# Cross-attention and RWKV block on one core: the permutation of the scan's output, on the moving read or on the PSUM write

## The chip, the cores and the metric

The kernel runs on one core of a Trainium2 chip, in one launch. The metric is the device time of an execution in microseconds, as a median over runs. Differences under 2% count as no change.

## What is computed

Two layers run one after the other for each of B = 4 batches. The first is a cross-attention with a small MLP, the second one is an RWKV block: a time mix with a recurrent scan over 256 tokens, then a channel mix. What the change touches is the output of the scan, which is then normalised per head. Cut to that part (b, l, e are batch, token and channel; h = 32 heads of s_ = 8 channels j):

```python
def step(s, rkvw):
    r_t, k_t, v_t, w_t = rkvw
    a = k_t[..., :, None] * v_t[..., None, :]
    out = jnp.einsum('bhi,bhij->bhj', r_t, u * a + s)
    s = a + w_t[..., :, None] * s
    return (s, out)
_, out = jax.lax.scan(step, s0, rkvw)
og = jnp.moveaxis(out, 0, 1).reshape(b, l, h, s_)
m = og.mean(-1, keepdims=True)
va = ((og - m) ** 2).mean(-1, keepdims=True)
og = ((og - m) / jnp.sqrt(va + 1e-05)).reshape(b, l, e) * gn_w + gn_b
x1 = x + og * g @ Wo.T
```

## The kernel before

All arithmetic around the change is in f32. Channels are 256 = 2 chunks of 128 partitions (index c), tokens are 256 = 2 row tiles of 128 (index a). The work is written as a list of steps, in an order set out by hand (ORDER, a string of stream names and counts): attention steps (maxima, exponentials, their products with V) of all batches are woven with the four "tails", one for each batch, a tail being the rest of the first layer and the whole second layer. Every engine walks the same list and takes its part of each step; semaphores order the engines among themselves. TensorE therefore runs its units strictly in the order of the list.

A tail unit writes one of two PSUM banks (pW), used in turn. A unit may start when the reader of the unit two places earlier has done with its bank (claim).

Around the change the steps are these. VectorE runs the scan as first-order recurrences (L897), VectorE and GpSimd multiply by the receptance r, and unit wkv (L622) sums over the channel i of every head on TensorE. That sum comes out with partitions (j4, h), that is four of the eight j with 32 heads each, in two halves jj, and tokens along the free axis. ScalarE copies it into the tile T (L778). Unit ojT then turns it around: its output has tokens on the partitions and the 256 channels along the free axis, in the order (h, j) that the rest of the layer uses. It does this with matmuls whose stationary operand is the data and whose moving operand is the identity, into one bank. For each row tile two matmuls put the diagonal term VT there (L632, plain 128x128 transposes, the first one clearing), and two more add the scan's halves (L635), where the channel order has to be changed from (j, h) to (h, j). VectorE then reads the bank: it sums each head's eight channels (gsum, L1099) and subtracts the mean (L1101, which releases the bank). ScalarE squares (L708), VectorE makes the variance and its inverse root (L1005, L1008, L904 to L915), and the layer goes on with the products of Wo.

What stands behind ojT on TensorE differs by batch. In batch 0 it is the transposes of Z of the next batch's tail (unit zT, L422) and then that tail's up projection (L549, with the down projection L558 behind it). In batches 1 and 2 the transposes zT of the next tail stand directly ahead of ojT and the up projection behind it. In batch 3 it is the last matmuls of the gate (L414). Tiles are named by the program: pW is the pair of banks, `four` holds VT, T holds the scan's sum, ident is the identity.

Of the kernel before, what the change touches and what calls it, by code (L numbers as in the profile page):

```python
# [7 lines left out]
P = 128  # L8
# [7 lines left out]
B, TQ, TC, E = 4, 256, 512, 256  # L16
# [7 lines left out]
H, S = 32, E // 32  # L24
# [133 lines left out]
def build(nc, hT, x, mask, cols, rows, ident_in, bsum_in, bfull_in, pick_in, w_kq, w_vo, w_up, w_down,  # L158
          w_maa1, w_maa2, w_td1, w_td2, w_sq, out):
    ctx = ExitStack()  # L160
    with ctx:
# [9 lines left out]
        ident = sb("ident", [P, P])  # L171
# [222 lines left out]
        def _(pe):  # L394
            mm = nc.tensor.matmul
# [31 lines left out]
            for step in STEPS:  # L427
# [48 lines left out]
                elif kind == "unit":  # L476
# [60 lines left out]
                    elif name == "zT":  # L537
                        pe.wait_ge(did["z"], b + 1)
                        transposes(name, b, X.Z)
                    elif name[:2] == "up":  # L540
                        if name == "up0":
                            taken(pe, "zT", b)
                            if b == 0:
                                pe.wait_ge(w_in["mlp"], 32)
                        bk = claim(name, b)
                        for i in range(2):
                            f = 2 * int(name[2]) + i
                            for c in range(C):
                                last = mm(bk[:, i * TQ:(i + 1) * TQ], Wup[:, c, f * P:(f + 1) * P], X.T[:, c, :],  # L549
                                          start=c == 0, stop=c == C - 1)  # L550
                        last.then_inc(unit_ready, 1)
                    elif name == "down":
                        bk = claim(name, b)
                        for a in range(QT):
                            for f in range(FC):
                                if a == 0 and f in (0, FC // 2):
                                    taken(pe, "up1" if f == 0 else "up3", b)
                                last = mm(bk[:, a * E:(a + 1) * E], X.U[:, f, a * P:(a + 1) * P], Wdown[:, f, :],  # L558
                                          start=f == 0, stop=f == FC - 1)
                        last.then_inc(unit_ready, 1)  # L560
                    elif name == "xaT":
                        pe.wait_ge(did["z2"], b + 1)
                        transposes(name, b, X.Z)
                    elif name == "maa1":
                        pe.wait_ge(did["xin"], b + 1)
                        if b == 0:
                            pe.wait_ge(w_in["maa"], 80)
                        bk = claim(name, b)
                        for c in range(C):
                            last = mm(bk[:, 0:TQ], Wmaa1[:, c, 0:P], X.T[:, c, :], start=c == 0, stop=c == C - 1)  # L570
                        last.then_inc(unit_ready, 1)
                    elif name == "maag":
                        bk = claim(name, b)
                        for c in range(C):
                            last = mm(bk[0:DM, 0:TQ], Wmaa1[:, c, P:NF * DM], X.T[:, c, :], start=c == 0, stop=c == C - 1)
                        last.then_inc(unit_ready, 1)
                    elif name[:4] == "mix_":
                        f = MIX[name[4]]
                        taken(pe, "maag" if f == 4 else "maa1", b)
                        bk = claim(name, b)  # L580
                        for c in range(C):
                            if f < 4:
                                lhs, rhs = Wmaa2[f * DM:(f + 1) * DM, c * P:(c + 1) * P], X.xob[f * DM:(f + 1) * DM, 0, :]
                            else:
                                lhs, rhs = Wmaa2g[:, c * P:(c + 1) * P], X.xob[0:DM, 1, :]
                            last = mm(bk[:, c * TQ:(c + 1) * TQ], lhs, rhs, start=True, stop=True)  # L586
                        last.then_inc(unit_ready, 1)
                    elif name in ("v", "k", "r", "g"):
                        if b == 0 and name == "v":
                            pe.wait_ge(w_in["sq"], 16)  # L590
                        pe.wait_ge(did["mix_" + name], b + 1)
                        square(name, b, Wsq[:, SQUARE.index("W" + name)], X.mixed[name], name == "g")
                    elif name == "td1":
                        pe.wait_ge(did["mix_w"], b + 1)
                        bk = claim(name, b)
                        for c in range(C):
                            last = mm(bk[0:DD, 0:TQ], Wtd1[:, c, :], X.mixed["w"][:, c, :],
                                      start=c == 0, stop=c == C - 1)
                        last.then_inc(unit_ready, 1)
                    elif name == "td2":  # L600
                        taken(pe, "td1", b)
                        bk = claim(name, b)
                        for c in range(C):
                            last = mm(bk[:, c * TQ:(c + 1) * TQ], Wtd2[:, c * P:(c + 1) * P], X.TH[0:DD, 0, :],
                                      start=True, stop=True)
                        last.then_inc(unit_ready, 1)
                    elif name == "diag":

                        pe.wait_ge(did["ruk"], b + 1)
                        bk = claim(name, b)  # L610
                        for c in range(C):
                            last = mm(bk[:, c * TQ:(c + 1) * TQ], bfull[:], X.RUK[:, c, :], start=True, stop=True)
                        last.then_inc(unit_ready, 1)
                    elif name == "wkv":

                        bk = claim(name, b)
                        for jj in range(S // 4):
                            for c in range(C):
                                pe.wait_ge(did[f"p{c}{jj}"], (b + 1) * (2 if jj == 0 else 1))
                            for c in range(C):  # L620
                                for j4 in range(4):
                                    last = mm(bk[32 * j4:32 * j4 + 32, jj * TQ:(jj + 1) * TQ], bsum[:, c, :],  # L622
                                              X.PR[c][:, 4 * jj + j4, :], start=c == 0, stop=c == C - 1)
                        last.then_inc(unit_ready, 1)
                    elif name == "ojT":
                        taken(pe, "diag", b)
                        taken(pe, "wkv", b)
                        bk = claim(name, b)
                        for a in range(QT):
                            for c in range(C):  # L630
                                at = a * E + c * P
                                mm(bk[:, at:at + P], X.VT[:, c, a * P:(a + 1) * P], ident[:], start=c == 0, stop=False)  # L632
                            by_head = bk[:, a * E:(a + 1) * E].rearrange("p (h j) -> p h j", j=S)
                            for jj in range(S // 4):
                                last = mm(by_head[:, :, 4 * jj:4 * jj + 4], X.T[:, jj, a * P:(a + 1) * P],  # L635
                                          ident[:].rearrange("p (j h) -> p h j", j=4), start=False, stop=jj == S // 4 - 1)
                        last.then_inc(unit_ready, 1)
                    elif name == "ogT":
                        pe.wait_ge(did["gg"], b + 1)
                        transposes(name, b, X.SX)  # L640
                    elif name == "wo":
                        taken(pe, "ogT", b)
                        square(name, b, Wsq[:, SQUARE.index("Wo")], X.T, True)
                    elif name == "xcT":
                        pe.wait_ge(did["z3"], b + 1)
                        transposes(name, b, X.Z)
                    elif name == "rr":
                        pe.wait_ge(did["xr"], b + 1)
                        square(name, b, Wsq[:, SQUARE.index("Wfr")], X.RT, True)
                    elif name == "kk":  # L650
                        pe.wait_ge(did["xk"], b + 1)
                        square(name, b, Wsq[:, SQUARE.index("Wfk")], X.KT, False)
                    elif name == "fv":
                        pe.wait_ge(did["kk"], b + 1)
                        square(name, b, Wsq[:, SQUARE.index("Wfv")], X.VT, True)
# [514 lines left out]
```

## Time and profile before

| what | value |
|---|---|
| median of 3 runs | 532.79 us (532.39 to 741.87) |
| profiled execution | 532.36 us |
| its span, first to last instruction | 530.6 us |
| mean granted TensorE clock over the span | 0.916 |
| TensorE (PE) busy | 442.5 us, 83% |
| VectorE (DVE) busy | 328.6 us, 62% |
| ScalarE (ACT) busy | 213.2 us, 40% |
| GpSimd (POOL) busy | 111.8 us, 21% |

All times below are from the one profiled execution and start at its first instruction. PE rows are matmuls, PEld rows the loads of their stationary operands, which overlap the matmuls. The duration of a matmul record reaches from its start to its modelled end, and records overlap, so the pace of a group is read from the starts of its first record and of the next group. A granted clock of 1.00 is 2.4 GHz, 0.50 is 1.2 GHz.

### The profile page before, as it was taken

To read this page: it belongs to the slowest core of one execution; us is meant where nothing else is said; L and a number is where in the kernel's file an instruction comes from. 1 tells how busy PE (TensorE), PEld (TensorE's weight loads), DVE (VectorE), ACT (ScalarE), POOL (GpSimd) and SP (SyncE) were. 2 spreads that over 40 slices of the span, in tenths; PEclk is the share of its full clock that TensorE was granted. 3 is DMA by queue.
4 is the path that set the end of the run, shared out by engine and by line. 5 is a ranking of instruction groups with operands and counts; after the bars stand their busy time and mean duration, and the time that the engine had idled before them with its cause. 6 is when DMAs were issued, how large, how long until landed. Compare 5 with 4: busy or idle time off the path is not lost.

```text
span 530.6 us, 7006 instructions
## 1 busy us (share of the span) xinstructions
PE 442.5 (83%) x2628; PEld 266.0 (50%) x2628; DVE 328.6 (62%) x592; ACT 213.2 (40%) x409; POOL 111.8 (21%) x103
## 2 busy tenths in 40 slices
PE   4988888888989989889989989899999796860655
PEld 2652243434765444467644544675564584540444
DVE  1257666563347577846768788447797444399653
ACT  1440065566425436541443547336368431130202
POOL 7330231300000041301004102402054300063400
PEclk9996599999999989999996999999999997575869
DMA  7889965554002722200062103000611000330001
GB/s 255 278 265 366 316 180 180 157 151 111 1 0 74 168 60 62 61 1 1 20 160 61 41 20 101 2 0 1 148 32 41 2 0 0 94 85 0 0 1 40
DMA packets 24696, 46.91 MB, mean 88 GB/s; under 512 B 2484, under 2 KB 18772, under 8 KB 23256
## 3 DMA queue, kind: packets, MB, share of 16 engines
q1 hardware_dynamic: 23672, 44.94, 29.5%
q10 hardware_dynamic: 992, 1.54, 0.9%
q8 instruction: 21, 0.34, 0.3%
q14 instruction: 11, 0.09, 0.1%
HBM read 31.63 MB, written 14.68 MB: 87 GB/s over the span
## 4 chain that ended last, share of the span: by engine, by line
PE 64%; DVE 23%; ACT 7%; issue 4%; DMA 1%; POOL 1%; SPq 0%; DVEq 0%; ACTq 0%; POOLq 0%
PE pW L414 10%; DVE mx L932 9%; PE pO L473 8%; PE pMX L441 7%; PE pST L456 7%; PE pW L558 5%; PE pW L549 5%; PE pW L586 4%; PE pW L487 4%; ACT probs L678 4%; DVE A L897 4%; PE pW L500 3%; PE pW L422 2%; PE pW L635 1%; DVE A L1052 1%
## 5 line engine op out<-in xcount | busy, mean ns | idle before, releaser
L932 DVE TENSOR_REDUCE mx<-pMX 128x1 f32<-128x512 f32 (+1 forms) x192 | 122.9, 685 | 43.7 <-PE pMX L441 42.5
L678 ACT ACTIVATE probs<-pST 128x512 f32<-128x512 f32 x192 | 103.9, 597 | 50.0 <-PE pST L456 48.7
L441 PE MATMUL pMX<-Kst,Qst 97*128 97x512 bf16 (+1 forms) x256 | 73.4, 358 | 22.9 <-DVE mx L932 21.6
L473 PE MATMUL pO<-probs,Vn 128*32 128x256 f32 x768 | 62.6, 398 | 0.9 <-ACT probs L678 0.4
L456 PE MATMUL pST<-Qst,Kst 99*128 99x256 bf16 x384 | 59.8, 279 | 0.8 <-ACT probs L678 0.8
L441 PEld LDWEIGHTS pMX<-Kst,Qst 97*128 97x128 bf16 x256 | 21.1, 100 | 68.9 <-DVE mx L932 53.9
L897 DVE TENSOR_TENSOR_SCAN A<-four,COL,A 128x256 f32<-128x256 f32 x64 | 49.7, 838 | 0.0
L456 PEld LDWEIGHTS pST<-Qst,Kst 99*128 99x128 bf16 x384 | 32.4, 99 | 34.2 <-ACT probs L678 16.5
L487 PE MATMUL pW<-hT,Wkq 128*128 128x256 f32 (+1 forms) x96 | 33.6, 502 | 7.4 <-DMA Wkq<-w_kq 7.1
L549 PE MATMUL pW<-T,Wup 128*128 128x256 f32 x128 | 29.0, 381 | 1.8 <-DVE SX L1101 1.2
L1087 DVE SCALAR_TENSOR_TENSOR A<-pW,COL,SX 128x256 f32<-128x256 f32 x32 | 14.0, 479 | 25.3 <-PE pW L586 25.3
L487 PEld LDWEIGHTS pW<-hT,Wkq 128*128 128x128 f32 x96 | 19.2, 207 | 20.4 <-issue 8.0
L1052 DVE SCALAR_TENSOR_TENSOR A<-pW,COL,A 128x256 f32<-128x256 f32 (+1 forms) x24 | 13.0, 570 | 26.3 <-ACT A L724 20.1
L558 PE MATMUL pW<-Wdown,four 128*128 128x256 f32 x128 | 28.3, 379 | 0.0
L414 PE MATMUL pW<-A,Wsq 128*128 128x256 f32 x96 | 26.5, 425 | 1.6 <-DVE A L959 1.6
L810 POOL TENSOR_TENSOR A<-A 128x1024 bf16<-128x1024 f32 x8 | 17.0, 2129 | 48.5 <-ACT A L692 48.5
L473 PEld LDWEIGHTS pO<-probs,Vn 128*32 128x32 f32 x768 | 15.2, 108 | 23.7 <-issue 14.8
L549 PEld LDWEIGHTS pW<-T,Wup 128*128 128x128 f32 x128 | 24.0, 190 | 5.9 <-ACT T L750 1.4
L842 POOL TENSOR_TENSOR Z<-Z,XA 128x512 f32<-128x512 f32 x4 | 6.3, 1583 | 97.0 <-DVE Z L1087 97.0
L558 PEld LDWEIGHTS pW<-Wdown,four 128*128 128x128 f32 x128 | 24.3, 190 | 3.3
L500 PE MATMUL pW<-Wvo,hT 128*128 128x256 f32 x96 | 24.3, 404 | 1.0 <-DVE A L1052 1.0
L414 PEld LDWEIGHTS pW<-A,Wsq 128*128 128x128 f32 x96 | 19.8, 216 | 7.1 <-DVE A L959 2.3
(135 smaller groups left out, 599.0 us busy)
## 6 DMA issues: line engine op xcount, KB each, us to landing
Kst<-k_stack SPq DMA_DIRECT2D x16, 576.0 KB
A<-v_rows SPq DMA_DIRECT2D x8, 1024.0 KB, 9.0
k_stack<-A SPq DMA_DIRECT2D x8, 576.0 KB, 3.1
k_stack<-A SPq DMA_DIRECT2D x8, 384.0 KB, 2.9
Qst<-q_stack SPq DMA_DIRECT2D x16, 192.0 KB
hT<-hT SPq DMA_DIRECT2D x3, 768.0 KB, 4.8
q_stack<-A SPq DMA_DIRECT2D x16, 128.0 KB, 3.1
Wsq<-w_sq SPq DMA_DIRECT2D x1, 2048.0 KB, 14.0
```

Of the source, the lines that this page charges most:

```text
L414: last = mm(bk[:, m * 256:(m + 1) * 256], lhs, rhs, start=c == 0, stop=c == C - 1)
L441: last = mm(pMX[n % 2][:, at:at + hi - lo], Qst[s][0:R_MASK + 1, h, qt * P:(qt + 1) * P], Kst[s][0:R_MASK + 1, h, lo:hi], start=True, stop ...
L456: last = mm(pST[n % ST_BANKS][:, i, :], Kst[s][0:R_LO + 1, h, nt * P:(nt + 1) * P], Qst[s][0:R_LO + 1, h, :], start=True, stop=True)
L473: last = mm(pO[32 * j:32 * j + 32, 0:TQ], Vn[b % 2][:, at:at + 32], probs[(n + j // 2) % UNITS_P][:, j % 2, :], start=nt == 0, stop=nt == ...
L487: last = mm(bk[:, at:at + hi - lo], Wkq[:, w, kc, c * P:(c + 1) * P], hb[:, kc, lo:hi], start=kc == 0, stop=kc == C - 1)
L500: last = mm(bk[:, i * E:(i + 1) * E], hb[:, kc, nt * P:(nt + 1) * P], Wvo[:, 0, kc, :], start=kc == 0, stop=kc == C - 1)
L549: last = mm(bk[:, i * TQ:(i + 1) * TQ], Wup[:, c, f * P:(f + 1) * P], X.T[:, c, :], start=c == 0, stop=c == C - 1)
L558: last = mm(bk[:, a * E:(a + 1) * E], X.U[:, f, a * P:(a + 1) * P], Wdown[:, f, :], start=f == 0, stop=f == FC - 1)
L586: last = mm(bk[:, c * TQ:(c + 1) * TQ], lhs, rhs, start=True, stop=True)
L678: act_fn(probs[n % UNITS_P][:], pST[n % ST_BANKS][:], ACT.Exp, scale=1.0 / DH)\
L897: last = v.tensor_tensor_scan(X.KV[c][:, j, :], X.WD[:, c, :], X.KV[c][:, j, :], COL[:, at + j:at + j + 1], ALU.mult, ALU.add)
L932: v.tensor_reduce(dst, src, AX.X, ALU.max).then_inc(max_done, 1)
```

## The change

One line of the matmul that adds the scan's halves, and the view it writes through. Before, the output view has the heads outside and four neighbouring j inside, and the moving identity is read in the same order (h, j), which takes its columns 32 apart. After, output and identity both go j outside and h inside: the identity's columns are read one after the other, and the output goes to every eighth column of the bank. The same values reach the same places. The order of the instructions on each engine, and their number, are the same in both kernels; on TensorE the 16 instructions of L635 have the output 128x32x4 before and 128x4x32 after.

```diff
-                            by_head = bk[:, a * E:(a + 1) * E].rearrange("p (h j) -> p h j", j=S)
+                            by_head = bk[:, a * E:(a + 1) * E].rearrange("p (h j) -> p j h", j=S)
                             for jj in range(S // 4):
-                                last = mm(by_head[:, :, 4 * jj:4 * jj + 4], X.T[:, jj, a * P:(a + 1) * P],
-                                          ident[:].rearrange("p (j h) -> p h j", j=4), start=False, stop=jj == S // 4 - 1)
+                                last = mm(by_head[:, 4 * jj:4 * jj + 4, :], X.T[:, jj, a * P:(a + 1) * P],
+                                          ident[:].rearrange("p (j h) -> p j h", j=4), start=False, stop=jj == S // 4 - 1)
```

## Rows read from the trace of the kernel before

**Rows 1.** The page's first lines: the span, busy time of the engines.
```profile
span 530.6 us, 7006 instructions
PE 442.5 (83%) x2628; PEld 266.0 (50%) x2628; DVE 328.6 (62%) x592; ACT 213.2 (40%) x409; POOL 111.8 (21%) x103
```

**Rows 2.** The page's chain that ended last, shares of the span by engine and line.
```profile
PE 64%; DVE 23%; ACT 7%; issue 4%; DMA 1%; POOL 1%; SPq 0%; DVEq 0%; ACTq 0%; POOLq 0%
PE pW L414 10%; DVE mx L932 9%; PE pO L473 8%; PE pMX L441 7%; PE pST L456 7%; PE pW L558 5%; PE pW L549 5%; PE pW L586 4%; PE pW L487 4%; ACT probs L678 4%; DVE A L897 4%; PE pW L500 3%; PE pW L422 2%; PE pW L635 1%; DVE A L1052 1%
```

**Rows 3.** Line L635: ns min/median/max, first and last start; who waited (us, times).
```profile
L635 PE MATMUL pW<-ident,T x32: 382/398/405, 229.6 to 500.1; 128*128 128x128 f32 x32
...
  DVE gsum L1099: 11.4, 4
```

**Rows 4.** Line L632, the same columns.
```profile
L632 PE MATMUL pW<-ident,four x32: 273/275/348, 229.1 to 499.4; 128*128 128x128 f32 x32
```

**Rows 5.** Line L422, the plain transposes of Z, the same columns.
```profile
L422 PE MATMUL pW<-ident,Z x48: 270/273/473, 135.0 to 518.0; 128*128 128x128 f32 x48
```

**Rows 6.** Timeline of PE around ojT of batch 0: start us, us, instruction, count.
```profile
229.10 0.68 PE L632 MATMUL pW<-ident,four 128*128 128x128 f32 x4 [0.90 <-issue]
229.62 1.04 PE L635 MATMUL pW<-ident,T 128*128 128x128 f32 x4
230.49 0.62 PE L632 MATMUL pW<-ident,four 128*128 128x128 f32 x4
230.95 1.05 PE L635 MATMUL pW<-ident,T 128*128 128x128 f32 x4
231.82 0.62 PE L422 MATMUL pW<-ident,Z 128*128 128x128 f32 x4
233.59 0.67 PE L549 MATMUL pW<-T,Wup 128*128 128x256 f32 x2 [1.16 <-DVE SX L1101]
```

**Rows 7.** Timeline of PE around ojT of batch 3.
```profile
497.62 0.68 PE L632 MATMUL pW<-ident,four 128*128 128x128 f32 x4 [0.77 <-issue]
498.13 1.06 PE L635 MATMUL pW<-ident,T 128*128 128x128 f32 x4
499.01 0.62 PE L632 MATMUL pW<-ident,four 128*128 128x128 f32 x4
499.48 1.06 PE L635 MATMUL pW<-ident,T 128*128 128x128 f32 x4
500.36 1.91 PE L414 MATMUL pW<-four,Wsq 128*128 128x256 f32 x8
```

**Rows 8.** Windows: length, PE, PEld, DVE, ACT, POOL busy, PEclk, DMA share, GB/s.
```profile
229.00:232.00 3.00, 2.90 (x18) 2.77 (x19) 0.61 (x2) 0.00 (x1) 0.61 (x1) 1.00 0.01 3
497.50:500.50 3.00, 2.88 (x17) 2.78 (x18) 0.31 (x1) 0.02 (x1) 0.00 (x0) 1.00 0.00 0
510.00:513.70 3.70, 3.54 (x8) 2.86 (x9) 0.00 (x0) 0.10 (x1) 0.00 (x0) 0.50 0.02 4
518.00:520.00 2.00, 2.00 (x11) 1.48 (x9) 0.60 (x1) 1.02 (x2) 0.00 (x0) 1.00 0.00 0
```

**Rows 9.** The chain in order of time, behind ojT of batch 0: start us, us.
```profile
232.03 0.70 DVE gsum L1099
...
232.76 0.70 DVE SX L1101
```

**Rows 10.** The same chain, around the end of ojT of batch 2.
```profile
424.27 0.88 PE pW L635 x4
425.15 2.85 PE pW L549 x13
```

**Rows 11.** The same chain, behind ojT of batch 3.
```profile
500.57 0.70 DVE gsum L1099
...
501.30 0.70 DVE SX L1101
...
502.02 0.64 ACT T L708
```

**Rows 12.** Timeline of VectorE and ScalarE beside ojT of batch 0.
```profile
229.64 0.61 DVE L938 TENSOR_SCALAR Z<-xob,rstd 128x256 f32<-128x256 f32 x2 [1.47 <-POOL rstd L802]
...
232.47 0.84 ACT L750 ACTIVATE T<-pW,COL 128x256 f32<-128x256 f32 x2 [3.47 <-PE pW L422]
```

**Rows 13.** Timeline of PE in the last 22 us.
```profile
508.35 1.11 PE L422 MATMUL pW<-ident,SX 128*128 128x128 f32 x4 [6.09 <-DVE SX L1020]
510.15 3.78 PE L414 MATMUL pW<-Wsq,T 128*128 128x256 f32 x8 [0.69 <-ACT T L747]
513.73 3.20 PE L414 MATMUL pW<-Wsq,four 128*128 128x256 f32 x8
...
518.14 1.89 PE L414 MATMUL pW<-Wsq,four 128*128 128x256 f32 x8
```

## The prediction, made before the changed kernel had run

> **What bounds the kernel now.** I read the page's first lines, then the chain that ended last, then the rows of the two lines that make up the unit ojT, then that unit's surroundings in time. The reader is to see first that TensorE is busy 83% of the span [rows 1], and that the chain runs through it for 64%; line L635, which is the line that changes, holds 1% of the chain [rows 2]. 1% of 530.6 us is about 5 us: that is the order of size of everything that follows, whichever way it goes.
>
> Then the lines. The profile has 32 records of L635 and 32 of L632 [rows 3, 4], although the program issues 16 of each (four batches, two row tiles, two per row tile): each of these f32 matmuls leaves two records. All have the same shape, 128x128 f32 from a 128-column identity, but L635 lasts 398 ns in the median and L632 275 ns. The same is seen for the plain transposes of L422, with 273 ns [rows 5]. So the extra 123 ns belongs to what L635 alone has, its two permuted patterns. These durations overlap, so the price is read from the starts. In batch 0 four records of L635 start at 229.62 and the next group at 230.49: 0.87 us, 218 ns each. The four of L632 behind them take from 230.49 to 230.95: 0.46 us, 115 ns each [rows 6]. In batch 3 it is 0.88 us against 0.47 us [rows 7]. Over the eight row tiles, of which rows 6 and 7 show the first two and the last two, the L635 groups sum to 7.00 us and the second-half L632 pace (0.4625 us on average) to 3.70 us. The clock does not explain it: the granted clock is 1.00, the 2.4 GHz level, in these stretches [rows 8].
>
> Last, who waits. VectorE's gsum reduction L1099 waits for L635 in all four batches, 11.4 us together [rows 3]. In batch 0 the chain goes from L635 straight through L1099 and L1101 into the up projection L549, which starts at 233.59 when L1101 releases its bank [rows 6, 9]. In batch 2 TensorE itself goes on without a gap, from L635 at 424.27 to L549 at 425.15 [rows 10]. In batch 3 everything behind is serial: L1099, L1101, ScalarE's square L708 [rows 11]. So in each of the four batches L635 lies on the path, not beside it.
>
> **The change part by part.** It removes the moving operand's permuted read. Before, the identity is read with the four j values innermost, 32 columns apart (128 bytes), so that each element read is far from the one before; the write has runs of four neighbours, one run every eight columns. After, the identity's 128 columns are read in order, and the write takes every eighth column (32 bytes apart), 32 heads for one j and then the next j. No instruction is added, none is moved, no wait is changed; on the other engines nothing changes, and SyncE's DMAs stay where they are. VectorE still reads the whole bank in order, so L1099 and L1101 keep their 0.70 us each.
>
> What the removed read is worth: if the 123 ns (by pace 103 ns) per record is the price of the read, and the write costs nothing more than it does now, a group of four falls from 0.875 us to 0.4625 us. That is 0.41 us for a row tile, 0.82 us for a batch, 3.30 us for the kernel, all of it on the path. What is late next? In batch 0 the transposes of Z (L422) follow L635 on TensorE, and ScalarE's copy of them ends just before L1101 does; both move forward together, and the Z they need was begun at 229.64 and took 0.61 us, so it stays ready 0.75 us ahead of the new start near 231.0 [rows 6, 12]. In batches 1 and 2 these transposes stand ahead of ojT, and up0 behind it. Nothing there waits on a transfer. I therefore take the whole 3.30 us and no discount.
>
> What the added write costs is not in this trace: no matmul here writes PSUM with a step, so it has to be bounded. From below, it is free: record pace 115 ns, the figure of L632, which writes in order. From above, take the opposite reading of the same rows: that the 103 ns is not a price of the read at all but of the breaks in the write, of which there are 32 in a record now (one per run of four). After the change there is one at each of 128 elements, which makes 4 x 103 + 115 = 527 ns a record, 309 ns more than now, and 32 x 309 = 9.9 us on the path. In between lies the case that read and write cost the same when the element beside is not taken: 218 ns as now, change 0. Of these I take the lower end. A record streams 128 elements in 115 ns, two such records per f32 matmul, so each output element gets 0.9 ns, and the row to which the new form is nearest is L632, which differs from it only in the step of its write.
>
> One rule speaks against this. The trace shows the price of broken patterns only for the read and write together, 218 against 115 ns [rows 6]. The Trainium skill, PSUM — Partial Sum Buffer, section Specifications (TRN2), gives PSUM 8-byte lines and says that "any non-contiguous AP slows matmuls significantly"; by its page SBUF — State Buffer (Door 1: The DMA port swizzle) the read wants at least two accesses to a 16-byte line. By both together the present form pays on the read and the new one on the write, and the gain of 3.30 us would shrink to nothing or turn. No run so far shows a stepped write by itself, so the rule becomes a rival below and not the forecast.
>
> The sum against the profiled execution, which took 532.36 us with a span of 530.6: 532.36 - 3.30 = 529.06. The median of the runs is 532.79, 0.43 above the profiled one, so the forecast is 529.5 us, 0.6% less than before. A difference of under 2% is about what a measurement of this kernel cannot tell from no change.
>
> **The rivals.**
> The write pays what the read paid. A stepped write loses the neighbour just as the stepped read does, 103 ns a record, and L635 stays near 218 ns. For it: the present form leaves the neighbour on the read side only, and its pace is close to half that of L632, a factor that a store could show just as well as a load. Against it: nothing in these rows separates the two. Time: 532.8, no change.
>
> The write pays per break (slower side). L635 goes to 527 ns a record, VectorE's L1099 waits 2.5 us longer in each batch, and the time is 532.8 + 9.9 = 542.7. For it: the write has breaks now as well, and the rows can't say which side costs the 103 ns. Against it: the write has three of its four steps in order now, and a break would have to cost 3.2 ns (103/32), seven columns' time at 2.4 GHz. It decides on the slower side from any record pace over 218 ns; it passes 2% (10.7 us) only from 218 + 333 = 551 ns. Smaller prices of the same kind, such as a doubling to 436 ns, give 32 x 218 = 7.0 us and 539.8.
>
> The gain is made and given back. L635 falls to 115 ns, but the clock behind it comes out otherwise. In batch 3's tail eight records of L414 take 3.58 us from 510.15 to 513.73 at a granted clock of 0.50, the 1.2 GHz level, after TensorE had been mostly idle while VectorE worked through its chain; later at 518.14, with the clock at 1.00, eight take 1.89 us [rows 8, 13]. One such group more or less at the lower level is 1.7 us, two of them are the gain. For it: a start 3.3 us earlier shifts where the clock falls and rises. Against it: the idle stretch before 508.35 is VectorE's own 6 us and does not change. Time: 531 to 533.
>
> That the change doesn't do what it says can be ruled out nearly: the 16 instructions change their output shape from 32x4 to 4x32 and stay in place.
>
> **How the numbers follow.** Free write: 0.46, 529.5 us, with its own range 528.5 to 530.5. Same price on the write: 0.30, 532.8. Given back: 0.08, 531 to 533. Price per break or a part of it: 0.16, from 534 to 542.7. The range begins at 528.5, a microsecond under the forecast for how the tail's clock falls, and reaches to 538.0: it takes in the first three cases and about a third of the last, and leaves out about one in ten. Faster by over 2% would need 10.7 us, when all of L635 holds 7.0: 0.01. Slower by over 2% needs more than the per-break price: 0.03. Within 2%: 0.96.
>
> **What would show it.** Right: L635's records last about 275 ns and stand 115 ns apart; the group between L632 and the next falls from 0.87 to 0.46 us; L1099's total wait falls by up to 3.3 us; the span ends near 527.3. If L635 stays near 398 ns and 218 ns apart, the write pays what the read paid. If its records last longer than 400 ns, the write's breaks are what costs. If L635 is short and the span hardly moves, I will look at the granted clock of the last 40 us, and at who waits between the batches. The prediction is wrong if the time is above 532, and its whole reason is wrong if L635 does not become shorter.

## The result, and the profile after

Six executions of the changed kernel took 525.92 us in the median (520.56 to 531.10), six of the kernel before 533.02 us. That is 7.1 us or 1.3%, within the 2% that count as no change, and twice the forecast gain; 525.92 lies under the predicted range. One execution of the kernel before, 741.87, is a stray; it counts in that median and in none of the means below. By plain means the difference is 6.0 us, with a standard error (the size by which chance alone moves it) of 2.2. The ratio given with the medians is 0.9847, with an interval from 0.9803 to 0.9891; it leaves out executions that lie more than 1.5% above the fastest of their kernel (here 530.04 and 531.10 of the changed kernel, and nine of twelve in the second repetition below, where it is 0.9849 again), and this kernel's executions spread more than that by themselves, so below the plain means are used.

L635's records, the whole of the change, came out as forecast. First the line's own rows in the changed kernel, with ns minimum, median and maximum [rows 3]:

```profile
L635 PE MATMUL pW<-ident,T x32: 275/275/275, 230.4 to 493.7; 128*128 128x128 f32 x32
...
  DVE gsum L1099: 8.0, 4
```

A record fell from 398 to 275 ns, L632's figure. VectorE's wait for it fell from 11.4 to 8.0 us in this execution. The timeline of TensorE and VectorE around ojT of batch 0 gives the pace [rows 6, 9]:

```profile
229.84 0.68 PE L632 MATMUL pW<-ident,four 128*128 128x128 f32 x4 [0.90 <-issue]
230.36 0.61 PE L635 MATMUL pW<-ident,T 128*128 128x128 f32 x4
230.80 0.61 PE L632 MATMUL pW<-ident,four 128*128 128x128 f32 x4
231.25 0.61 PE L635 MATMUL pW<-ident,T 128*128 128x128 f32 x4
231.70 0.60 PE L422 MATMUL pW<-ident,Z 128*128 128x128 f32 x4
231.90 0.69 DVE L1099 TENSOR_REDUCE gsum<-pW 128x64 f32<-128x512 f32 x1 [0.91 <-PE pW L635]
232.62 0.69 DVE L1101 SCALAR_TENSOR_TENSOR SX<-gsum,pW 128x512 f32<-128x512 f32 x1
```

Four records now take 0.44 and 0.45 us where they took 0.87: 111 ns a record, a little under the 115 taken for the free case. But ojT of batch 0 starts at 229.84, 0.74 us later than before, and the span is 524.0 us, 6.6 us shorter. So something else moved too. The windows between the starts of ojT of batches 0, 1, 2, 3 and the end show where. The columns are length, busy time of PE, PEld, DVE, ACT and POOL, granted clock, DMA share and GB/s. The kernel before:

```profile
229.10:339.31 110.21, 99.29 (x628) 61.12 (x629) 76.42 (x143) 47.97 (x94) 19.96 (x20) 0.95 0.20 49
339.31:422.30 82.99, 77.77 (x552) 49.88 (x550) 57.01 (x101) 43.81 (x86) 22.33 (x19) 1.00 0.15 36
422.30:497.62 75.32, 49.54 (x207) 34.34 (x205) 47.68 (x76) 15.52 (x29) 19.94 (x15) 0.73 0.14 32
497.62:530.60 32.98, 20.36 (x80) 16.08 (x80) 14.88 (x36) 5.79 (x10) 2.38 (x4) 0.84 0.05 16
```

The changed kernel, with the same columns:

```profile
229.84:337.44 107.60, 96.17 (x629) 59.83 (x629) 76.02 (x143) 47.95 (x94) 19.91 (x20) 0.98 0.20 50
337.44:419.52 82.08, 76.86 (x551) 49.17 (x550) 57.02 (x101) 43.79 (x86) 22.38 (x19) 1.00 0.15 36
419.52:491.93 72.41, 44.34 (x207) 31.74 (x205) 47.47 (x76) 15.50 (x29) 18.99 (x15) 0.79 0.14 33
491.93:524.00 32.07, 18.30 (x80) 14.54 (x80) 14.72 (x36) 5.78 (x10) 2.36 (x4) 0.89 0.05 17
```

The second stretch is the one to read: the clock is 1.00 in both, nothing in it differs but one ojT, and it is 0.91 us shorter. Four times that is 3.6 us, an estimate, since it reads one of the four batches. The first and third are 2.6 and 2.9 us shorter, and in both the clock is higher after. The mean granted clock of the whole span rose from 0.916 to 0.935, without the change having put any work elsewhere.

From here two theories. **Theory A:** the change is worth its 3.5 us, and the rest of the first difference is where the granted clock was low in the executions that were drawn. **Theory B:** the change itself moves the clock, so that about 7 us are its gain.

### The profile page after: what moved, and what is told of

Its sections match the earlier page's. It is cut to its first block, busy times and chain, and to the rows that moved or that the text cites. A ratio compares the mean times of both kernels' runs of the same rounds, so it can differ in the third digit from the quotient of the medians.

```text
span 524.0 us, 7006 instructions
## 1 busy us (share of the span) xinstructions
PE 431.6 (82%) x2628; PEld 259.9 (50%) x2628; DVE 327.8 (63%) x592; ACT 213.0 (41%) x409; POOL 110.8 (21%) x103
## 4 chain that ended last, share of the span: by engine, by line
PE 60%; DVE 24%; ACT 7%; issue 4%; DMA 3%; POOL 1%; SPq 0%; DVEq 0%; ACTq 0%; POOLq 0%
DVE mx L932 10%; PE pW L414 10%; PE pO L473 8%; PE pST L456 7%; PE pMX L441 6%; PE pW L558 5%; PE pW L549 5%; DVE A L897 4%; PE pW L487 4%; ACT probs L678 4%; PE pW L500 3%; PE pW L586 3%; PE pW L422 2%; DMA A<-v_rows 1%; DMA Wkq<-w_kq 1%
## 5 line engine op out<-in xcount | busy, mean ns | idle before, releaser
L441 PE MATMUL pMX<-Kst,Qst 97*128 97x512 bf16 (+1 forms) x256 | 72.6, 354 | 23.3 <-DVE mx L932 22.2
L473 PE MATMUL pO<-probs,Vn 128*32 128x256 f32 x768 | 62.5, 397 | 0.9 <-ACT probs L678 0.4
L456 PE MATMUL pST<-Qst,Kst 99*128 99x256 bf16 x384 | 59.4, 277 | 0.8 <-ACT probs L678 0.8
L441 PEld LDWEIGHTS pMX<-Kst,Qst 97*128 97x128 bf16 x256 | 20.9, 99 | 69.1 <-DVE mx L932 53.3
L897 DVE TENSOR_TENSOR_SCAN A<-four,COL,A 128x256 f32<-128x256 f32 x64 | 53.9, 904 | 0.0
L456 PEld LDWEIGHTS pST<-Qst,Kst 99*128 99x128 bf16 x384 | 32.3, 98 | 33.7 <-ACT probs L678 16.8
L422 PE MATMUL pW<-ident,Z 128*128 128x128 f32 x48 | 8.1, 294 | 24.2 <-DVE Z L948 22.4
L473 PEld LDWEIGHTS pO<-probs,Vn 128*32 128x32 f32 x768 | 15.2, 108 | 23.6 <-issue 14.7
L414 PE MATMUL pW<-A,Wsq 128*128 128x256 f32 x96 | 25.6, 413 | 1.6 <-DVE A L959 1.6
L842 POOL TENSOR_TENSOR Z<-Z,XA 128x512 f32<-128x512 f32 x4 | 4.4, 1089 | 94.6 <-DVE Z L1087 94.6
```

Of the source, the lines that this page charges most:

```text
L414: last = mm(bk[:, m * 256:(m + 1) * 256], lhs, rhs, start=c == 0, stop=c == C - 1)
L422: last = nc.tensor.transpose(bk[:, c * TQ + a * P:c * TQ + (a + 1) * P], src[:, a, c * P:(c + 1) * P], ident[:])
L441: last = mm(pMX[n % 2][:, at:at + hi - lo], Qst[s][0:R_MASK + 1, h, qt * P:(qt + 1) * P], Kst[s][0:R_MASK + 1, h, lo:hi], start=True, stop ...
L456: last = mm(pST[n % ST_BANKS][:, i, :], Kst[s][0:R_LO + 1, h, nt * P:(nt + 1) * P], Qst[s][0:R_LO + 1, h, :], start=True, stop=True)
L473: last = mm(pO[32 * j:32 * j + 32, 0:TQ], Vn[b % 2][:, at:at + 32], probs[(n + j // 2) % UNITS_P][:, j % 2, :], start=nt == 0, stop=nt == ...
L897: last = v.tensor_tensor_scan(X.KV[c][:, j, :], X.WD[:, c, :], X.KV[c][:, j, :], COL[:, at + j:at + j + 1], ALU.mult, ALU.add)
```

## Experiments

**The changed kernel again, twice.** No edit.

> The changed kernel once more, for more executions of both kernels. Theory A (the read's price plus chance): the four ojT units are 3.5 us shorter, as in the first profile, and the rest of the 7 us is where the granted clock happens to fall; then the executions of each kernel spread over about 6 us, and executions of the two kernels with the same mean clock differ by far less than 7 us. Pooled over all executions the changed kernel is 3 to 4 us faster. Theory B (the change itself moves the clock): the pooled difference stays near 7 us, and the changed kernel has about 20 us less of low clock in most executions.

> The changed kernel a third time, for more executions of both. Theory A: over this call's executions its mean is 3 to 4 us under that of the kernel before, give or take the 1.5 us that some ten executions with a spread of 4 us leave open; single executions fall anywhere between 520 and 532. Theory B (the change itself moves the clock): the means differ by 6 us or more.

Measured: the first repetition took 530.97 us in the median (six executions, 520.49 to 531.30), against 530.27 for eleven of the kernel before; the second 529.20 (twelve, 520.68 to 531.35) against 530.72 for 23. By their medians the same program that had won 7 us is 0.7 us slower in the first and 1.5 us faster in the second; by plain means it is 1.8 and 3.0 us faster. The windows of the first repetition, cut at its own ojT starts:

```profile
229.20:341.71 112.51, 101.58 (x628) 62.08 (x629) 76.41 (x143) 47.95 (x94) 19.94 (x20) 0.92 0.19 48
341.71:423.79 82.08, 76.86 (x551) 49.26 (x550) 57.01 (x101) 43.79 (x86) 22.13 (x19) 1.00 0.15 36
423.79:495.50 71.71, 43.62 (x206) 31.30 (x205) 47.50 (x76) 15.49 (x29) 18.94 (x15) 0.79 0.14 33
495.50:529.30 33.80, 20.36 (x80) 16.51 (x80) 14.69 (x35) 5.78 (x10) 2.37 (x4) 0.84 0.05 16
```

The second stretch is 82.08 us again, to the hundredth. The first is 112.51 in place of 107.60, with the clock at 0.92 in place of 0.98: 4.9 us between two executions of one program. One piece of it in the timeline of TensorE shows the same instructions at both levels. First the first profile of the changed kernel, then its repetition:

```profile
279.00 1.10 PE L586 MATMUL pW<-xob,Wmaa2g 32*128 32x256 f32 x4
...
280.56 0.64 PE L473 MATMUL pO<-probs,Vn 128*32 128x256 f32 x8
281.14 0.61 PE L456 MATMUL pST<-Qst,Kst 99*128 99x256 bf16 x4
```

```profile
280.00 1.10 PE L586 MATMUL pW<-xob,Wmaa2g 32*128 32x256 f32 x4
...
281.99 1.08 PE L473 MATMUL pO<-probs,Vn 128*32 128x256 f32 x8
283.01 1.03 PE L456 MATMUL pST<-Qst,Kst 99*128 99x256 bf16 x4
```

L473 and L456 stand behind the same small products of 32 and 64 rows (L586, L604) and in the repetition take 1.08 and 1.03 us instead of 0.64 and 0.61. TensorE had no gap in the 6 us ahead of them in either. In the first profile the clock fell as well, but later and for a shorter time. Windows of the first profile, then of the repetition, with the clock in the third column from the end:

```profile
279.00:285.00 6.00, 4.97 (x27) 1.92 (x27) 5.44 (x10) 2.55 (x5) 3.91 (x2) 1.00 0.52 133
286.00:288.00 2.00, 2.00 (x15) 1.11 (x8) 1.16 (x3) 0.67 (x2) 0.64 (x1) 0.50 0.04 8
```

```profile
281.00:294.00 13.00, 12.26 (x47) 5.43 (x46) 9.52 (x13) 3.09 (x6) 5.55 (x2) 0.50 0.23 62
```

The last stretch differs too. In the repetition batch 3's ojT ran at the lower level of the clock, which it did neither in the first profile nor in the kernel before. The window of that unit, two of its groups, and who waited for L635:

```profile
495.50:499.05 3.55, 3.54 (x17) 3.55 (x17) 0.00 (x0) 0.00 (x0) 0.00 (x0) 0.50 0.00 0
...
496.49 1.06 PE L635 MATMUL pW<-ident,T 128*128 128x128 f32 x4
497.34 1.06 PE L632 MATMUL pW<-ident,four 128*128 128x128 f32 x4
...
  DVE gsum L1099: 10.4, 4
```

Four records of L635 take 0.85 us there, nearly what the stepped read took at the upper level. The unit takes 3.55 us, where it took 2.74 in the kernel before [rows 7], and VectorE's wait is 10.4 us in place of 8.0. The profile of the second repetition has the same 10.4 us. So batch 3's part of the gain is not there in every execution.

Pooled over the whole study, 62 executions of the kernel before have a mean of 530.90 us (526.35 to 535.51) and 24 of the changed one 527.76 us (520.49 to 531.35). The difference is 3.14 us with a standard error of 0.84, so about 1.5 to 4.8 us, a ratio of 0.994. Theory A expected 3 to 4, theory B 6 or more; B falls, though a smaller part of the clock in these 3.1 us is not excluded. Executions of the same mean clock lie closer together, as A expected: at 0.935 three of the changed kernel average 525.85 us and four of the kernel before 527.51, at 0.919 five and four average 531.14 and 532.09. That is less than 3 us; batch 3's lost part fits it, but the rest was not followed up.

**As long as before, but with the read in order.** Two superfluous matmuls are put ahead of each row tile's first one.

```diff
-                                mm(bk[:, at:at + P], X.VT[:, c, a * P:(a + 1) * P], ident[:], start=c == 0, stop=False)
+                                for n, start in enumerate((True,) * 3 if c == 0 else (False,)):
+                                    mm(bk[:, at:at + P], X.VT[:, c, a * P:(a + 1) * P], ident[:], start=start, stop=c == 0 and n < 2)
```

> The changed kernel with two superfluous plain transposes ahead of each row tile's first one, whose result is overwritten: 4 records of 115 ns, 0.46 us a row tile, 3.7 us in all, as long as what the change took away. Theory A: about 3.7 us slower than the changed kernel over its executions, so level with the kernel before, about 532. Theory B in the form that the place of the tail against the scan or the transfers matters: the same, 532. Theory C (the strided read does something more, for instance it holds up others that read the same memory, or its slow matmuls count less for the clock): it stays under 530, since the time is back but the strided read is not.

Measured: 531.64 us in the median of six, mean 530.88, against a mean of 530.81 for the eleven executions of the kernel before that were measured with it; ratio 1.0001 (0.9949 to 1.0054). With a standard error of 1.1 us the mean alone would not rule out theory C's 530. The stretch from batch 1's ojT to batch 2's does, with the clock at 1.00:

```profile
338.13:421.10 82.97, 77.75 (x559) 50.06 (x558) 57.04 (x101) 43.82 (x86) 22.14 (x19) 1.00 0.14 36
```

It takes 82.97 us, against 82.99 in the kernel before, although the read is in order. Putting the TensorE time back at the same place takes the gain away, whatever the time is spent on, so theory C, by which the strided read does something more, falls; its form about the clock is not tested by this stretch.

**Read and write apart.** Three kernels set the two patterns of L635 one at a time. Each writes the channels in an order other than the reference's.

```diff
 # plain read, plain write
+ mm(bk[:, a * E + jj * P:a * E + (jj + 1) * P], X.T[:, jj, a * P:(a + 1) * P], ident[:], ...)
 # stepped read, plain write
+ plain = bk[:, a * E + jj * P:a * E + (jj + 1) * P].rearrange("p (h j) -> p h j", j=4)
+ mm(plain, X.T[:, jj, a * P:(a + 1) * P], ident[:].rearrange("p (j h) -> p h j", j=4), ...)
 # plain read, write in runs of four
+ mm(by_head[:, :, 4 * jj:4 * jj + 4], X.T[:, jj, a * P:(a + 1) * P], ident[:].rearrange("p (h j) -> p h j", j=4), ...)
```

> L635 reads the identity in order and writes 128 neighbouring columns, so the channels stay in the order (j, h); left out is the permutation. If the step in the write is free, L635 keeps 275 ns and a group of four 0.44 to 0.46 us, as after. If the write's step costs something, the records become shorter than 275 ns or stand closer than 111 ns.

> L635 reads the identity 32 columns apart, as before, and writes 128 neighbouring columns; the output order is another one than the reference's. If the read was the price: 398 ns a record and 0.87 us a group of four, as before. If the runs of four in the write were the price: 275 ns and 0.46 us.

> L635 reads the identity in order and writes in runs of four, as before; the channels come out in another order than the reference's. If the read was the whole price, 275 ns a record and 0.44 us a group of four. If the breaks in the write had a part in it, between 275 and 398 ns.

Measured: 275 ns with both plain, 275 ns with the write in runs of four, and the old price with the stepped read alone. The timeline of TensorE at batch 1's ojT, with the stepped read:

```profile
343.58 1.06 PE L636 MATMUL pW<-ident,T 128*128 128x128 f32 x4
344.47 0.62 PE L632 MATMUL pW<-ident,four 128*128 128x128 f32 x4
```

and with both plain:

```profile
342.25 0.61 PE L635 MATMUL pW<-ident,T 128*128 128x128 f32 x4
342.70 0.61 PE L632 MATMUL pW<-ident,four 128*128 128x128 f32 x4
```

That is 0.89 us against 0.45 for a group of four. Single executions carry no verdict on their times (531.13, 532.90 and 530.04 us), but the stretch from batch 1's ojT to batch 2's does, since the clock is 1.00 there in all of them. First the stepped read, then both plain:

```profile
343.13:426.12 82.99, 77.77 (x551) 49.87 (x550) 57.03 (x101) 43.82 (x86) 22.14 (x19) 1.00 0.15 36
```

```profile
341.81:423.89 82.08, 76.86 (x551) 49.17 (x550) 57.02 (x101) 43.82 (x86) 22.54 (x19) 1.00 0.15 36
```

82.99 is the figure of the kernel before, 82.08 that of the changed one. The traces of all the other runs without padding and without a change to L441 agree: 82.98 or 82.99 us with the stepped read (four), 82.08 or 82.09 with the plain one (seven). So the stepped read was the whole price, 0.91 us for eight records or 114 ns each, and the step of 32 bytes in the write costs nothing that can be seen: a plain write is not faster.

**The steps in a faster stream.** Two kernels put the step on the 512-column bf16 matmuls of the row maxima (L441), once on the write and once on the read; a maximum does not ask for the order.

```diff
 # stepped write
+ if i < QT: dst, keys = dst.rearrange("p (h j) -> p j h", j=8), keys.rearrange("p (j h) -> p j h", j=8)
 # stepped read
+ if i < QT: dst, keys = dst.rearrange("p (h j) -> p h j", j=4), keys.rearrange("p (j h) -> p h j", j=4)
```

> The changed kernel with the step put on the write of the two 512-column maximum matmuls of each head as well (L441, bf16, every eighth column, 128 of the 256 records; a maximum doesn't ask for the order). They stream one element in 0.42 ns, against 0.9 ns in L635. If a stepped write is free at any pace, a 512-column record stays near its 358 to 430 ns. If it is free in L635 only because the f32 matmul is slow, these records get longer, up to twice the streaming time (about 215 ns more).

> The changed kernel with the stepped read put on the moving operand of the two 512-column bf16 maximum matmuls of each head (L441, 128 columns apart, runs of four in the write, 128 of the 256 records). If a read without a neighbour costs 1.7 ns per element at any type (218 ns for 128 in L635 of before), a record takes about 870 ns plus its end, over 1000 ns. If it costs a factor of two over the streaming time, about 630 ns, as the stepped write did (634 ns in place of 414 to 420).

The groups of that line with shapes kept apart: instructions, busy time, mean ns of one, idle time before them and its releaser. The changed kernel, the stepped write, the stepped read:

```profile
L441 PE MATMUL pMX<-Kst,Qst 97*128 97x512 bf16 x128 | 49.9, 414 | 14.5 <-DVE mx L932 13.7
```

```profile
L444 PE MATMUL pMX<-Kst,Qst 97*128 97x512 bf16 x128 | 76.1, 634 | 10.9 <-DVE mx L934 10.7
```

```profile
L444 PE MATMUL pMX<-Kst,Qst 97*128 97x512 bf16 x128 | 125.3, 1031 | 8.1 <-DVE mx L934 8.0
```

By these means a record with the stepped write is 220 ns longer, one with the stepped read 617 ns. So the write is not free at any pace. The means mix both levels of the clock, so the pace is read from starts at a granted clock of 1.00, in the timeline of TensorE. The changed kernel, the stepped write, the stepped read:

```profile
275.84 0.61 PE L441 MATMUL pMX<-Kst,Qst 97*128 97x512 bf16 x2
276.28 0.60 PE L456 MATMUL pST<-Qst,Kst 99*128 99x256 bf16 x4
```

```profile
193.73 1.03 PE L444 MATMUL pMX<-Kst,Qst 97*128 97x512 bf16 x2
194.56 0.64 PE L458 MATMUL pST<-Qst,Kst 99*128 99x256 bf16 x4
```

```profile
186.88 1.03 PE L444 MATMUL pMX<-Kst,Qst 97*128 97x512 bf16 x1
187.73 3.63 PE L502 MATMUL pW<-Wvo,hT 128*128 128x256 f32 x16
```

Two plain matmuls of 512 columns take 0.44 us, 0.43 ns an element. Two with the stepped write take 0.83 us, 0.81 ns an element, a little under the 0.87 that L635 takes anyway (111 ns for 128). That fits a stepped write which L635's f32 matmul is slow enough to hide; no run shows the reason itself. One stepped read takes 0.85 us, 1.66 ns an element, which is close to the 1.70 that L635 showed before (218 ns for 128). At the lower level of the clock the stepped read takes the same time. The row, and the windows of this read and of the one above:

```profile
69.41 1.04 PE L444 MATMUL pMX<-Kst,Qst 97*128 97x512 bf16 x1
...
69.41:70.27 0.86, 0.86 (x2) 0.31 (x1) 0.65 (x1) 0.00 (x0) 0.86 (x1) 0.50 0.47 112
186.88:187.73 0.85, 0.85 (x2) 0.19 (x1) 0.65 (x1) 0.00 (x0) 0.00 (x0) 1.00 0.00 0
```

These two kernels took 539.51 and 619.54 us, one execution each.

**Keeping the clock up near the end.** Superfluous matmuls stand in two stretches in which TensorE waits for VectorE; n is 32 and 10, then 24 and 13.

```diff
+            def warm(name, b, n):
+                bk = claim(name, b)
+                for _ in range(n):
+                    mm(bk[:, 0:E], ident[:], Wsq[:, 0, 0, :], start=True, stop=True)
...
+                        if b == 3:   # ahead of the wait in ogT; the same with b == 2 in xcT
+                            warm(name, b, n)
```

> The changed kernel with superfluous f32 matmuls (128x256, 0.43 us each at the full clock) in two stretches near the end in which TensorE waits for VectorE: 32 ahead of the transposes of batch 2's last normalised rows, 10 ahead of batch 3's ogT. Their result is overwritten. Theory A (the spread and the part of the first difference beyond 3.5 us is where the granted clock happens to be low): the clock stays at 1.00 from about 470 us to the end, the work behind the two stretches is 3 to 5 us shorter than in the second profile of the changed kernel, the median falls to 523 to 526, and executions spread less than 11 us. If the low clock is not what costs: no change, or slower by what the fillers overrun.

> The kernel before with the same fillers. Theory A: the same gain of 3 to 5 us over its own executions, and with part of the chance gone it is 3 to 4 us slower than the changed kernel with fillers. Theory B (the change acts through the clock): the two with fillers are within 1 us, or still 7 us apart.

Measured: 528.79 us in the median of twelve (522.55 to 529.35) for the changed kernel with fillers, mean 528.24; 529.44 for the one before with fillers, mean 528.83. Two expectations failed. The changed kernel did not get faster, and the two differ by 0.6 us with a standard error of 0.9, not by 3 to 4. A part of the first is in the timeline of the changed kernel with fillers:

```profile
489.94 0.70 DVE L957 TENSOR_SCALAR Z<-xob,mv,rstd 128x256 f32<-128x256 f32 x2
...
492.45 0.60 PE L427 MATMUL pW<-ident,Z 128*128 128x128 f32 x4
```

The rows were ready at 490.64 and their transposes began at 492.45: the fillers ran 1.8 us over. In the kernel before they ran over by 1.6 us, so this does not explain why the two are level. The fillers did lift the clock: the last stretch took 31.02 us at 0.94, where the repetition's took 33.80 at 0.84, but the stretch before it grew from 71.71 to 73.90. Eleven of the twelve executions of the changed one lie within 1.7 us of each other, those of the kernel before over 8 us: the low stretches do not fall alike in the two programs. So the second run had fewer fillers.

> The changed kernel with 24 fillers ahead of the first stretch (32 ran 1.8 us past the rows they waited for) and 13 ahead of the second. Theory A: 2 us faster than with 32 and 10 fillers, so a mean near 526, with less spread than the changed kernel without fillers has.

> The kernel before with the same 24 and 13 fillers. Theory A: 3 to 4 us slower in the mean than the changed kernel with the same fillers, near 529.5. Theory B: level with it, or 6 us slower.

Measured: means 525.21 us (six executions, 517.97 to 528.59; ratio to the kernel before 0.9848, 0.9784 to 0.9912) and 528.44 us (twelve, 524.75 to 533.05). They differ by 3.2 us, with a standard error of 1.8. The clock of the changed one's last 44 us:

```profile
480.00:524.00 44.00, 34.00 (x183) 27.28 (x181) 28.89 (x54) 7.40 (x13) 8.72 (x9) 0.97 0.04 12
```

It is 0.97, and this is the fastest version of the study by its mean, 5.7 us under the kernel before over all executions. Against the changed kernel without fillers it is 2.6 us, with a standard error of 1.8, so the gain of the fillers in the mean is not settled. Stage by stage it can be seen. The last two stretches of its profile, from batch 2's ojT on:

```profile
423.80:493.27 69.47, 55.02 (x254) 41.67 (x253) 46.38 (x75) 15.51 (x29) 18.12 (x15) 0.88 0.15 34
493.27:523.10 29.83, 21.61 (x106) 17.74 (x106) 16.23 (x37) 5.78 (x10) 3.26 (x5) 1.00 0.05 18
```

They are 2.2 and 4.0 us shorter than in the repetition of the changed kernel, whose first two stretches are as long as here (112.51 and 82.08 there, 112.50 and 82.09 here). The spread did not shrink as expected: the low clock between batches 0 and 1 is still there.

## Why the prediction was right and wrong

- *The extra 123 ns belongs to L635's permuted patterns, and it is the read.* Right. The stepped read alone brings it back, the plain write takes nothing off, the runs of four cost nothing.
- *Record pace 115 ns, 0.41 us a row tile, 3.30 us for the kernel, all on the path.* Right for batch 1, and a little small: 111 ns, and 0.91 us in the stretch with a steady clock, which would make 3.6 us for four batches. *No discount* was wrong for batch 3, whose ojT ran at the lower clock in two of three profiles of the changed kernel and took longer than before. The pooled means differ by 3.14 us (1.5 to 4.8).
- *The write is free because each element gets 0.9 ns.* It is free, and the bf16 runs fit the reason: with 0.43 ns an element the same step makes the record half as long again. The rival that the write pays what the read paid would have been right there in kind.
- *By the rule of the Trainium skill (PSUM — Partial Sum Buffer, Specifications (TRN2)) the stepped write slows the matmul significantly.* Wrong for this f32 matmul, 275 ns with and without the step. It holds for the bf16 one, 634 against 414 ns.
- *VectorE's wait falls by up to 3.3 us.* Right in the first profile, 3.4 us; in the two repetitions it fell by 1.0 us, with batch 3's ojT at the lower clock.
- *The range from 528.5, a microsecond under the forecast for how the tail's clock falls; the given-back case as 531 to 533.* This step failed. I priced the clock at one or two groups of L414, 1.7 us each, in the last 22 us, and allowed it 1 us on the fast side. The kernel's own executions spread over 520.5 to 531.4 us after and 526.4 to 535.5 before, mostly by the clock between batches 0 and 1 (4.9 us between two profiles of one program) and after batch 2 (6.2 us with fillers against the repetition without). The fastest executions lie 9 us under the forecast. The page's clock line had the low slices and the 0.916 in it, but I read the granted clock in four short windows only.
- *The median 532.79 as the base.* This failed with it: three executions, two of which agreed within 0.4 us, were no base. The mean of 62 is 530.90, and on that the same 3.30 us give 527.6, where the changed kernel's mean is 527.76. That the two agree so closely is partly luck, since the difference has a standard error of 0.84 us and batch 3's part of the 3.30 was lost in some executions. So was 525.92: the median of 24 is 529.47.

## What to carry to other kernels

When a matmul against the identity must permute, put the step on the PSUM write and let the moving operand be read in order: here the stepped read doubled an f32 matmul's time and the stepped write added nothing. In a bf16 matmul both cost, the write less. Only steps of 128 and 256 bytes on the read and of 32 bytes on the write were run. And before a range is written, look at how the granted clock lies over the whole span: where it is low in several places, agreement of three executions says little, and a gain of a few microseconds is read from a stretch with a steady clock.

## What the runs showed of the hardware that was not expected

- A stepped read of the moving operand costs about the same per element in f32 (218 ns for 128, 1.70 ns) and bf16 (0.85 us for 512, 1.66 ns), so it takes twice the time of the plain stream in f32 and four times in bf16 (0.43 ns).
- In bf16 the stepped read takes the same at both levels of the clock, 0.86 us for 512 columns at 0.50 and 0.85 at 1.00. For f32 no stepped read was seen at the lower level; the plain L635 took 0.85 us for four records there, against 0.87 for the stepped one at the upper.
- A write of every eighth f32 column took 0.81 ns an element behind a bf16 matmul and added nothing to an f32 matmul, which takes 0.87 ns.
- The granted clock fell to the 1.2 GHz level behind matmuls of 32 and 64 rows although TensorE had no gap in the 6 us before; in another execution of the same program the same instructions ran at 2.4 GHz, and the clock fell later and for a shorter time. What decides when it falls was not found, nor why the kernels with 32 and 10 fillers came out level.
